# Six units' fronts of a graph layer's edge loop moved into the mixing stage

## The chip, the cores and the metric

One core of one Trainium2 chip runs the whole kernel in one launch. The metric is the device time of an execution in microseconds (us); the median over runs is compared. The kernel is written in Bass: each engine (TensorE, VectorE, ACT, GpSimd, and SyncE, which only issues transfers) has its own instruction list and runs it in order, and engines wait for each other on semaphores.

## What is computed

A graph layer in float32 on 3125 nodes with 256 channels and 50000 edges sorted by their destination: a message layer over the edges, an attention-like mixing, and a mixture of experts. What matters here:

```python
xn  = layernorm(x)
msg = silu(concat(xn[src], xn[dst], w) @ mW1 + mb1)        # edge loop, front
msg = layernorm(msg) * g + b                               # statistics: front; scaling: back
msg = silu(msg @ mW2 + mb2)                                # back
agg = segment_sum(msg, src, N)                             # back
y   = silu(concat(xn, agg) @ uW1 + ub1) @ uW2 + ub2        # hpre = xn @ uW1[:256] + ub1
mix = (q @ (k^T v)) / N @ Wout + bout                      # folded: mixed = xn @ mixG
x   = x + xn + y + mix                                     # then the experts
```

(The kernel's `near` side is the node whose block a tile of edges shares, `dst_table` holds the other side.)

## The kernel before, in words

Nodes are 25 blocks of 125. The product of `xn` with the near half of `mW1` stands in SBUF (`src_hi`, `src_lo`, high and low part), that with the far half in the DRAM table `dst_table`. The matrices of attention are folded into one 256x256 matrix `mixG`.

**Mixing stage** (TensorE L1004 to L1024). Blocks come in seven chunks `CH` of 4, 4, 4, 4, 4, 4 and 1 (numbered 0 to 6). For each block TensorE makes `mixed` = xn @ mixG (six matmuls, banks 0 and 1 in turn), and waits from block 2 on for VectorE's addition of the block two back (L1695, L1696); behind the blocks of a chunk it makes `hpre` (twelve matmuls, banks 2 to 5, two a chunk), which ACT copies out with a bias (L1327 to L1333). From chunk 2 on TensorE waits for the copy of the chunk two back. GpSimd meanwhile issues the twelve gathers of units 0 to 5 (L777 to L780), waits for the end of mixing, clears `agg` (L783, over `xnT_lo`, which mixing reads) and only then starts its part of the loop. SyncE writes `row_list` and `weight_rows` to DRAM (L597 to L601), waits for these (L602) and for `w2_lo` (L603), which VectorE writes after mixing (L1758, L1759), and then loads `near_rows` and the weight rows of `hotT`, five units at a time (L604 to L614). `near_rows` lies over `w2c`, from which `w2_hi` and `w2_lo` are made.

**Edge loop** (an `edge_step(n, k, ...)` on each engine, L1033, L1335, L1701 and `edge_pair` L767). 212 units of 2x128 edges. Step n does, in this order on each engine:

- TensorE: tr, the transposes of unit n-6; the second-layer products of n-7; the near products of unit n (four matmuls that pick rows of `src_hi` and `src_lo` by the one-hot `hotT`, L1069, bank 1 or 2); the sums of n-8.
- ACT: copy of the transposes (n-6), SiLU in place on `msg1` (n-1, L1346), scaling `msg1n` (n-5, L1353), SiLU of the second layer (n-7, L1360).
- VectorE: `hotT` of unit n+1 (L1708), shifts `nw_b` of a pair (n-4), the first addition into `agg` (n-9), `msg1T_lo` (n-6), the second addition (n-9), statistics of n-1 (L1743), the addition of the near products of unit n to the gathered far rows (L1748), the one-hot `hot` (n-7).
- GpSimd, for pairs m, m+1: waits for both units' statistics (`spread_ok`), an addition and a power (L748, L750), then the four gathers of units m+6 and m+7.

The first 20 units and the last are written out, between them runs a hardware loop of ten units a turn. Before the loop TensorE waits for `w2_lo`, for all 25 additions of mixing and for all hpre copies.

The front of a unit is its `hotT`, near products, addition, SiLU and statistics; none of them touches `agg`, `msg1n`, or banks 3 to 6 and 0 and 7, which the back half uses. Before, the front of units 0 to 5 ran alone, ahead of the first tr.

## Time and profile before

| what | value |
|---|---|
| three runs | 1538.51, 1540.53 (median), 1542.70 us |
| the profiled execution | 1532.65 us, its span 1530.9 us, mean granted clock of TensorE 0.918 |
| busy, share of the span | TensorE 85%, its weight loads 74%, VectorE 75%, ACT 59%, GpSimd 57% |
| chain that ended last | TensorE 51%, VectorE 15%, ACT 11%, "issue" 10%, unknown 7% |
| mixing stage | 370.5 to 413.7 us from the start |
| first near product, first transposes of the loop | 419.45 and 431.07 us |

PE is TensorE, PEld its weight loads, DVE VectorE, POOL GpSimd, SP SyncE. A row of the timeline gives start, duration, engine, line, operation, output<-inputs, shape and count, and in brackets how long the engine had been idle and what ended that. A releaser "remote" or "another core or an unknown queue" is none that the profile knows; "issue" is an engine that waited for nothing the profile shows. A clock of 1.00 is TensorE's upper level (2.4 GHz), 0.50 its lower one (1.2 GHz).

### The profile page before, as it was taken

The page shows a single profiled execution, that of the slowest core. Times are in us where ns is not written, and L with a number is a line of the kernel's source. Part 1 is how long each engine was busy: PE and PEld are TensorE (multiplying, and loading weights), DVE is VectorE, ACT ScalarE, POOL GpSimd, SP SyncE. Part 2 cuts the span into 40 slices and gives each one's busy share as a digit, 9 for nine tenths or more (in the row PEclk, how much of TensorE's full clock was granted, in tenths as well). Part 3 has the DMA queues.
Part 4 walks back from the last instruction along what each step waited for, and adds up shares of the span by engine and source line. Part 5 has one row for each costly group of instructions (what it writes and reads, how often), then busy time and mean ns, then how long its engine had stood idle before and what let it go on. Part 6 is the DMA issues. An engine that isn't in the chain of part 4 may idle for free.

```text
span 1530.9 us, 31977 instructions
## 1 busy us (share of the span) xinstructions
PE 1302.3 (85%) x8639; PEld 1135.4 (74%) x8640; DVE 1154.1 (75%) x2784; ACT 904.1 (59%) x1796; POOL 866.8 (57%) x960
## 2 busy tenths in 40 slices
PE   2576727998789999999999999999998956999991
PEld 1365626887678888888888888888886745888891
DVE  6975815884279989999999999999994678766662
ACT  1843603442257777777777777777774553666660
POOL 2287870002277777777777777777760012676761
PEclk7676967998879999999999999999999987999996
DMA  3911100001123333333333333333354143444447
GB/s 131 163 27 25 43 14 8 15 3 41 41 87 103 94 93 93 93 102 97 90 93 93 102 93 94 92 95 100 94 66 165 41 149 138 66 72 75 73 64 265
DMA packets 69786, 129.87 MB, mean 85 GB/s; under 512 B 22626, under 2 KB 43424, under 8 KB 69095
## 3 DMA queue, kind: packets, MB, share of 16 engines
q0 software_dynamic: 35408, 74.18, 20.5%
q1 hardware_dynamic: 33538, 51.70, 11.7%
q10 hardware_dynamic: 780, 3.24, 0.5%
q8 instruction: 31, 0.51, 0.1%
q14 instruction: 29, 0.24, 0.1%
HBM read 103.71 MB, written 25.22 MB: 84 GB/s over the span
## 4 chain that ended last, share of the span: by engine, by line
PE 51%; DVE 15%; ACT 11%; issue 10%; another core or an unknown queue 7%; DMA 3%; DVEq 1%; ACTq 1%; POOLq 0%; SPq 0%
PE ps L840 9%; ACT msg1n_t L1353 7%; PE ps L1079 5%; PE ps L1057 3%; PE ps L1052 3%; PE ps L1053 3%; PE ps L1069 3%; PE ps L1180 2%; DVE place_val_t L1591 2%; PE ps L1209 2%; PE ps L1211 2%; PE ps L1210 2%; PE ps L1181 2%; PE ps L1182 2%
## 5 line engine op out<-in xcount | busy, mean ns | idle before, releaser
L763 POOL DMA_INDIRECT msg_t<-dst_table,stage_idx x424 | 422.7, 997 | 121.1 <-issue 119.5
L1052 PE MATMUL ps<-w_hi_t,msg1T_hi_t 128*128 128x256 f32 x848 | 239.3, 304 | 0.0
L1353 ACT ACTIVATE msg1n_t<-msg_t,nw_b,nw_y 128x256 f32<-128x256 f32 x424 | 229.3, 591 | 0.0
L1079 PE MATMUL ps<-msg_t,hot_t 128*125 128x256 f32 x848 | 222.4, 384 | 2.0 <-issue 0.9
L1053 PE MATMUL ps<-w_lo_t,msg1T_hi_t 128*128 128x256 f32 x848 | 221.6, 283 | 0.0
L1360 ACT ACTIVATE msg_t<-ps 128x512 f32<-128x512 f32 x212 | 125.5, 592 | 124.0 <-remote 100.6
L1748 DVE TENSOR_TENSOR msg_t<-ps,msg_t 128x512 f32<-128x512 f32 x212 | 144.4, 681 | 63.3 <-remote 59.4
L1726 DVE TENSOR_TENSOR agg_t<-agg_t,ps 125x256 f32 x424 | 173.6, 409 | 6.8 <-PE ps L1079 3.4
L1057 PE MATMUL ps<-w_hi_t,msg1T_lo_t 128*128 128x256 f32 x848 | 171.0, 283 | 0.0
L1053 PEld LDWEIGHTS ps<-w_lo_t,msg1T_hi_t 128*128 128x128 f32 x848 | 163.1, 192 | 0.0
L1341 ACT ACTIVATE msg1T_hi_t<-ps 128x512 fp32r<-128x512 f32 x212 | 126.4, 596 | 60.4 <-PE ps L840 56.0
L1052 PEld LDWEIGHTS ps<-w_hi_t,msg1T_hi_t 128*128 128x128 f32 x848 | 161.9, 191 | 0.0
L1079 PEld LDWEIGHTS ps<-msg_t,hot_t 128*125 128x125 f32 x848 | 143.4, 187 | 21.0 <-issue 6.4
L840 PEld LDWEIGHTS ps<-ident,msg1n_t 128*128 128x128 f32 x848 | 97.4, 141 | 75.6 <-ACT msg1n_t L1353 52.4
L840 PE MATMUL ps<-ident,msg1n_t 128*128 128x128 f32 x848 | 134.6, 282 | 21.7 <-ACT msg1n_t L1353 19.1
L729 POOL DMA_INDIRECT sorted_edges<-sort_sb_t,chunk_to x112 | 128.0, 1143 | 37.3 <-issue 32.6
L1743 DVE BATCH_NORM_STATS2 est<-msg_t 128x6 f32<-128x512 f32 x212 | 147.5, 696 | 2.1 <-ACT msg_t L1346 2.1
L1735 DVE SCALAR_TENSOR_TENSOR msg1T_lo_t<-ps,msg1T_hi_t 128x512 fp32r<-128x512 f32 x212 | 144.4, 681 | 4.6 <-issue 2.4
L1346 ACT ACTIVATE msg_t<-msg_t 128x512 f32<-128x512 f32 x212 | 133.7, 631 | 12.4 <-DVE msg_t L1748 11.4
L1057 PEld LDWEIGHTS ps<-w_hi_t,msg1T_lo_t 128*128 128x128 f32 x848 | 132.1, 192 | 0.0
L1069 PE MATMUL ps<-src_hi_t,hotT_t 127*128 x424 | 114.3, 290 | 8.4 <-DVE hotT_t L1708 8.4
L831 POOL DMA_INDIRECT total<-slot_z,to_row x56 | 88.6, 1582 | 48.9 <-ACT slot_z L1433 44.3
(373 smaller groups left out, 3098.8 us busy)
## 6 DMA issues: line engine op xcount, KB each, us to landing
near_rows<-row_list SPq DMA_DIRECT2D x42, 320.0 KB
w_sb_t<-in_L_ffn_W_dram SPq DMA_DIRECT2D x16, 512.0 KB, 8.7
msg_t<-dst_table,stage_idx POOLq DMA_INDIRECT x424
res_t<-in_x_dram SPq DMA_DIRECT2D x1, 3125.0 KB
total<-zero_chunks_t SPq DMA_DIRECT2D x1, 3125.0 KB
dst_table<-dst_stage SPq DMA_DIRECT2D x25, 125.0 KB
xm_table<-xm_t POOLq DMA_DIRECT2D x5, 625.0 KB, 7.6
sum_a_t<-total SPq DMA_DIRECT2D x5, 625.0 KB, 10.7
```

The source lines that it names most:

```text
L763: pool.indirect_dma_start(out=msg1[:, k, j, :], out_offset=None, in_=dst_table, in_offset=bass.IndirectOffsetOnAxis(stage_idx[:, G * k + j ...
L840: return pe.transpose(out_, in_, ident[0:rows, 0:rows])
L1052: pe.matmul(o[j], part(msg1T_hi, j, c), w2_hi[:, c, :], start=(c == 0), stop=False)
L1053: pe.matmul(o[j], part(msg1T_hi, j, c), w2_lo[:, c, :], start=False, stop=False)
L1057: m = pe.matmul(o[j], part(msg1T_lo, j, c), w2_hi[:, c, :], start=False, stop=(c == KD - 1))
L1069: m = pe.matmul(bank(1 + k % 2, D, first=j * D), hotT[0:HR, k, j * 128:j * 128 + 128], table[0:HR, bass.ts(blk[k, j], 1), :].rearrange("p ...
L1079: m = pe.matmul(bank(7 * (kl % 2), D, rows=NP, first=j * D), hot[:, kl % 2, j, 0:NP], msg2[:, kl % 2, j, :], start=True, stop=True)
L1353: m = A(msg1n[:, (kl + 1) % 2, j, :], msg1[:, kk, j, :], ACT.Identity, bias=nw_b[:, kk, j:j + 1], scale=nw_y[:, kk, j:j + 1])
L1726: dve.tensor_tensor(a, a, bank(7 * ((k + 1) % 2), D, rows=NP, first=j * D), ALU.add).then_inc(sum_sb, 1)
L1735: dve.scalar_tensor_tensor(msg1T_lo[:, k % 2], bank(3 + k % 2), 1.0 / ROOT_D, msg1T_hi[:, k % 2].bitcast(F32), ALU.add, ALU.subtract).then ...
L1743: dve.bn_stats(est_pairs[:, kk, :], msg1[:, kk].rearrange("p j n -> p n j")).then_inc(spread_ok, 1)
L1748: dve.tensor_tensor(v, bank(1 + k % 2), v, ALU.add).then_inc(pre_sb, 1)
```

## The change

The fronts of units 0 to 5 are issued within mixing: unit 0 in chunk 2, units 1 and 2 in chunk 3, 3 and 4 in chunk 4, 5 in chunk 5 (`FRONT`), on TensorE between the chunk's mixed and hpre products, on VectorE behind the chunk's additions, on ACT ahead of the chunk's hpre copy, but for unit 5's step there (SiLU of unit 4, scaling of unit 0), which stays behind the last copy. Mixing takes banks 0 and 7, hpre 3 to 6, so that 1 and 2 are the near products' own. `w2_hi` and `w2_lo` are made ahead of mixing, and TensorE waits for them there. GpSimd does its first two pairs (units 0 to 3) before it waits for the end of mixing and clears `agg`. Only positions, waits and bank numbers change; every product, addition and transfer is the same.

```diff
--- before.py
+++ after.py
@@ -462,6 +462,8 @@
         N_DST = [(NB + 1) // 2, NB // 2]
         SMALL = 9
         CH = [list(range(t, min(t + 4, NB))) for t in range(0, NB, 4)]
+        EARLY = 6
+        FRONT = {c: {2: [0], 3: [1, 2], 4: [3, 4], 5: [5]}.get(c, []) for c in range(len(CH))}
         LAST = UNITS + 9 + LAG
         FROM = 2
         PEEL = (UNITS // TURN - 1) * TURN
@@ -778,11 +780,12 @@
                 stage(m, m, 0)
             for m in range(AHEAD_UNITS):
                 gather(m)
-            pool.wait_ge(hpre_ps, len(CH))
-            pool.wait_ge(mixed_ps, NB)
-            pool.memset(agg[:], 0.0).then_inc(fills, 1)
             pool.wait_ge(token_ok, 1)
             for m in range(0, FROM * TURN, 2):
+                if m == EARLY - 2:
+                    pool.wait_ge(hpre_ps, len(CH))
+                    pool.wait_ge(mixed_ps, NB)
+                    pool.memset(agg[:], 0.0).then_inc(fills, 1)
                 edge_pair(m, m % TURN, m // TURN)
             with pool.Fori(FROM, UNITS // TURN - 1) as i:
                 st.enter(i, FROM, len(PARTS) + TURN // 2)
@@ -1001,33 +1004,6 @@
                 m.then_inc(mixG_ps, 1)
 
 
-            pe.wait_ge(w_lo_ok, MIXG_LO)
-            for c, blocks in enumerate(CH):
-                t0, nb = blocks[0], len(blocks)
-                for t in blocks:
-                    if t >= 2:
-                        pe.wait_ge(mixed_ok, t - 1)
-                    o = bank(t % 2, D, rows=NP)
-                    for k in range(KD):
-                        pe.matmul(o, xnT_hi[:, t, k, 0:NP], mixG_hi[:, k, :], start=(k == 0), stop=False)
-                        pe.matmul(o, xnT_hi[:, t, k, 0:NP], mixG_lo[:, k, :], start=False, stop=False)
-                        m = pe.matmul(o, xnT_lo[:, t, k, 0:NP], mixG_hi[:, k, :], start=False, stop=(k == KD - 1))
-                    m.then_inc(mixed_ps, 1)
-                if c >= 2:
-                    pe.wait_ge(hpre_sb, c - 1)
-                for f in range(KD):
-                    o, F = bank(2 + 2 * (c % 2) + f, nb * 128), slice(f * 128, f * 128 + 128)
-                    for k in range(KD):
-                        pe.matmul(o, uw1x_hi[:, k, F], xnT_hi[:, t0:t0 + nb, k, :], start=(k == 0), stop=False)
-                        pe.matmul(o, uw1x_lo[:, k, F], xnT_hi[:, t0:t0 + nb, k, :], start=False, stop=False)
-                        m = pe.matmul(o, uw1x_hi[:, k, F], xnT_lo[:, t0:t0 + nb, k, :], start=False, stop=(k == KD - 1))
-                m.then_inc(hpre_ps, 1)
-
-
-            pe.wait_ge(w_lo_ok, W2_LO)
-            pe.wait_ge(bw_in, 128)
-            pe.wait_ge(mixed_ok, NB)
-            pe.wait_ge(hpre_sb, len(CH))
             blk = {}
 
             def edge_step(n, k, turn_weights):
@@ -1080,7 +1056,35 @@
                                       start=True, stop=True)
                     m.then_inc(sum_ps, 1)
 
-            for n in range(FROM * TURN):
+            pe.wait_ge(w_lo_ok, W2_LO)
+            pe.wait_ge(bw_in, 128)
+            for c, blocks in enumerate(CH):
+                t0, nb = blocks[0], len(blocks)
+                for t in blocks:
+                    if t >= 2:
+                        pe.wait_ge(mixed_ok, t - 1)
+                    o = bank(7 * (t % 2), D, rows=NP)
+                    for k in range(KD):
+                        pe.matmul(o, xnT_hi[:, t, k, 0:NP], mixG_hi[:, k, :], start=(k == 0), stop=False)
+                        pe.matmul(o, xnT_hi[:, t, k, 0:NP], mixG_lo[:, k, :], start=False, stop=False)
+                        m = pe.matmul(o, xnT_lo[:, t, k, 0:NP], mixG_hi[:, k, :], start=False, stop=(k == KD - 1))
+                    m.then_inc(mixed_ps, 1)
+                if c >= 2:
+                    pe.wait_ge(hpre_sb, c - 1)
+                for n in FRONT[c]:
+                    edge_step(n, n % TURN, 16)
+                for f in range(KD):
+                    o, F = bank(3 + 2 * (c % 2) + f, nb * 128), slice(f * 128, f * 128 + 128)
+                    for k in range(KD):
+                        pe.matmul(o, uw1x_hi[:, k, F], xnT_hi[:, t0:t0 + nb, k, :], start=(k == 0), stop=False)
+                        pe.matmul(o, uw1x_lo[:, k, F], xnT_hi[:, t0:t0 + nb, k, :], start=False, stop=False)
+                        m = pe.matmul(o, uw1x_hi[:, k, F], xnT_lo[:, t0:t0 + nb, k, :], start=False, stop=(k == KD - 1))
+                m.then_inc(hpre_ps, 1)
+
+
+            pe.wait_ge(mixed_ok, NB)
+            pe.wait_ge(hpre_sb, len(CH))
+            for n in range(EARLY, FROM * TURN):
                 edge_step(n, n % TURN, 16 * (n // TURN) + 16)
             with pe.Fori(FROM, UNITS // TURN - 1) as i:
                 for k in range(TURN):
@@ -1323,15 +1327,6 @@
             for c in range(KD):
                 act.wait_ge(mixG_ps, c + 1)
                 A(mixG_hi[:, c, :], bank(2 + c, D), ACT.Copy, scale=1.0 / N).then_inc(mixG_sb, 1)
-            act.wait_ge(small_in, 16 * SMALL)
-            for c, blocks in enumerate(CH):
-                act.wait_ge(hpre_ps, c + 1)
-                for f in range(KD):
-                    m = A(hpre[:, blocks[0]:blocks[0] + len(blocks), f, 0:NP],
-                          bank(2 + 2 * (c % 2) + f, len(blocks) * 128).rearrange("p (i n) -> p i n", n=128)[:, :, 0:NP],
-                          ACT.Identity, bias=ub1_col[:, f:f + 1])
-                m.then_inc(hpre_sb, 1)
-
             def edge_step(n, k, turn_rows):
                 late, kl = n - LAG, (k - LAG) % TURN
                 m_ = late - 6
@@ -1360,8 +1355,20 @@
                     A(msg2[:, (kl + 1) % 2].rearrange("p j n -> p (j n)"), bank(5 + (kl + 1) % 2), ACT.Silu)\
                         .then_inc(msg2_sb, 1)
 
+            act.wait_ge(small_in, 16 * SMALL)
+            for c, blocks in enumerate(CH):
+                for n in FRONT[c]:
+                    if n < EARLY - 1:
+                        edge_step(n, n % TURN, 32)
+                act.wait_ge(hpre_ps, c + 1)
+                for f in range(KD):
+                    m = A(hpre[:, blocks[0]:blocks[0] + len(blocks), f, 0:NP],
+                          bank(3 + 2 * (c % 2) + f, len(blocks) * 128).rearrange("p (i n) -> p i n", n=128)[:, :, 0:NP],
+                          ACT.Identity, bias=ub1_col[:, f:f + 1])
+                m.then_inc(hpre_sb, 1)
+
             pairs = 0
-            for n in range(FROM * TURN):
+            for n in range(EARLY - 1, FROM * TURN):
                 edge_step(n, n % TURN, 32 * ((n - LAG) // TURN) + 32)
             with act.Fori(FROM, UNITS // TURN - 1) as i:
                 pairs = TURN // 2 * i
@@ -1691,10 +1698,9 @@
                 dve.wait_ge(mixG_sb, c + 1)
                 dve.scalar_tensor_tensor(mixG_lo[:, c, :], bank(2 + c, D), 1.0 / N, mixG_hi[:, c, :].bitcast(F32),
                                          ALU.mult, ALU.subtract).then_inc(w_lo_ok, 1)
-            for t in range(NB):
-                dve.wait_ge(mixed_ps, t + 1)
-                dve.tensor_tensor(res[R, t, :], res[R, t, :], bank(t % 2, D, rows=NP), ALU.add).then_inc(mixed_ok, 1)
-
+            step(dve.tensor_scalar(w2_hi[:], w2c[:], ROOT_D, None, ALU.mult))
+            dve.scalar_tensor_tensor(w2_lo[:], w2c[:], ROOT_D, w2_hi[:].bitcast(F32), ALU.mult, ALU.subtract).then_inc(w_lo_ok, 1)
+            dve.wait_ge(table_sb, LOADS)
 
             blk = {}
 
@@ -1753,14 +1759,17 @@
                     dve.tensor_tensor(hot[:, (k + 1) % 2, :, 0:NP], iota[:, 1:NP + 1].unsqueeze(1).broadcast_to([128, G, NP]),
                                       rows.broadcast_to([128, G, NP]), ALU.is_equal).then_inc(hot_ready, 1)
 
-            dve.wait_ge(mixG_sb, KD)
-
-            step(dve.tensor_scalar(w2_hi[:], w2c[:], ROOT_D, None, ALU.mult))
-            dve.scalar_tensor_tensor(w2_lo[:], w2c[:], ROOT_D, w2_hi[:].bitcast(F32), ALU.mult, ALU.subtract).then_inc(w_lo_ok, 1)
-            dve.wait_ge(table_sb, LOADS)
             near_of = lambda n: 16 * ((n + 1) // TURN) + 16
             pairs = 0
-            for n in range(-1, FROM * TURN):
+            for c, blocks in enumerate(CH):
+                for t in blocks:
+                    dve.wait_ge(mixed_ps, t + 1)
+                    dve.tensor_tensor(res[R, t, :], res[R, t, :], bank(7 * (t % 2), D, rows=NP), ALU.add).then_inc(mixed_ok, 1)
+                for n in FRONT[c]:
+                    if n == 0:
+                        edge_step(-1, TURN - 1, -1, near_of(-1), 0)
+                    edge_step(n, n % TURN, n // TURN, near_of(n), 32)
+            for n in range(EARLY, FROM * TURN):
                 edge_step(n, n % TURN, n // TURN, near_of(n), 32 * (n // TURN) + 32)
             with dve.Fori(FROM, UNITS // TURN - 1) as i:
                 pairs = TURN // 2 * i
```

## Rows read from the trace of the kernel before

**Rows 1.** Busy time by stage: us; PE, PEld, DVE, ACT, POOL; PEclk; DMA

```profile
500.00:534.00 34.00, 33.06 (x234) 29.33 (x233) 31.70 (x75) 25.55 (x51) 25.72 (x31) 1.00 0.32 95
```

**Rows 2.** Timeline of TensorE between mixing and the loop

```profile
413.39 0.27 PE L1023 MATMUL ps<-xnT_lo_t,uw1x_hi_t 128*128 128x128 f32 x1
419.45 0.58 PE L1069 MATMUL ps<-src_hi_t,hotT_t 127*128 x1 [5.78 <-DVE hotT_t L1708]
431.07 1.12 PE L840 MATMUL ps<-ident,msg1n_t 128*128 128x128 f32 x4 [2.08 <-ACT msg1n_t L1353]
```

**Rows 3.** The same timeline, the other engines

```profile
413.21 0.69 DVE L1759 SCALAR_TENSOR_TENSOR w_lo_t<-w2c,w_hi_t 128x512 fp32r<-128x512 f32 x1
413.70 0.62 ACT L1330 ACTIVATE hpre_t<-ps,ub_col 128x125 f32<-128x125 f32 x2 [0.74 <-PE ps L1023]
413.73 5.43 POOL L783 MEMSET agg_t<- 128x6400 f32 x1 [26.14 <-PE ps L1023]
413.98 0.35 SPq L608 DMA_DIRECT2D near_rows<-row_list  x1
421.43 0.63 ACT L1346 ACTIVATE msg_t<-msg_t 128x512 f32<-128x512 f32 x1 [5.80 <-DVE msg_t L1748]
422.09 0.71 DVE L1743 BATCH_NORM_STATS2 est<-msg_t 128x6 f32<-128x512 f32 x1 [0.44 <-ACT msg_t L1346]
422.71 0.67 DVE L1748 TENSOR_TENSOR msg_t<-ps,msg_t 128x512 f32<-128x512 f32 x1
```

**Rows 4.** The line of hotT (L1708) in 413 to 420: duration ns min/median/max

```profile
L1708 DVE TENSOR_SCALAR hotT_t<-near_rows,row_col x2: 334/804/1274, 418.0 to 419.2; 125x256 fp32r<-125x256 f16 x2
```

**Rows 5.** Timeline of the mixing stage

```profile
370.41 7.27 SPq L600 DMA_DIRECT2D weight_rows<-side_w_t  x2
388.32 0.42 DVE L1696 TENSOR_TENSOR res_t<-res_t,ps 125x256 f32<-125x256 f32 x1 [8.13 <-remote]
388.80 0.57 PE L1012 MATMUL ps<-mixG_hi,xnT_hi_t 128*125 128x256 f32 x1 [5.31 <-DVE res_t L1696]
394.79 1.25 ACT L1330 ACTIVATE hpre_t<-ps,ub_col 128x500 f32<-128x500 f32 x2 [9.48 <-PE ps L1023]
408.76 0.39 PE L1021 MATMUL ps<-xnT_hi_t,uw1x_hi_t 128*128 128x512 f32 x1
408.96 0.42 DVE L1696 TENSOR_TENSOR res_t<-res_t,ps 125x256 f32<-125x256 f32 x1 [0.29 <-PE ps L1014]
411.51 0.28 PE L1012 MATMUL ps<-mixG_hi,xnT_hi_t 128*125 128x256 f32 x1
```

**Rows 6.** DMA queues (packets, MB, share) in 387:388, then in 388:392

```profile
q1 hardware_dynamic: 53, 0.03, 8.7%
...
q0 software_dynamic: 58, 0.16, 11.6%
```

**Rows 7.** Busy time by stage again, PEclk third from the end

```profile
391.00:392.00 1.00, 1.00 (x6) 1.00 (x5) 0.07 (x1) 0.00 (x0) 0.00 (x0) 0.50 0.00 0
392.00:393.00 1.00, 1.00 (x6) 0.78 (x6) 0.36 (x1) 0.00 (x0) 0.00 (x0) 1.00 0.00 0
...
414.00:419.00 5.00, 0.00 (x0) 0.00 (x0) 0.97 (x1) 1.61 (x3) 5.00 (x1) 0.69 0.42 135
```

**Rows 8.** Chain of waits: four near products at the lower and upper clock

```profile
438.04 0.85 PE ps L1069 x4
...
455.95 0.48 PE ps L1069 x4
```

**Rows 9.** TensorE's sequencer, loads of block numbers (L491), duration ns

```profile
L491 PEldq TENSOR_LOAD <-tile_blk x106: 328/332/527, 414.5 to 1141.3; - x106
```

**Rows 10.** The page's group of gathers: busy, mean ns, idle before

```profile
L763 POOL DMA_INDIRECT msg_t<-dst_table,stage_idx x424 | 422.7, 997 | 121.1 <-issue 119.5
```

**Rows 11.** Timeline in the loop: GpSimd's power and an addition beside it

```profile
693.65 1.04 POOL L750 TENSOR_TENSOR nw_y<-nw_v,minus_half 128x4 f32<-128x4 f32 x1
693.94 0.69 DVE L1748 TENSOR_TENSOR msg_t<-ps,msg_t 128x512 f32<-128x512 f32 x1 [0.71 <-remote]
```

## The prediction

> **What bounds the kernel now.** In what follows near(u), silu(u) and add(u) are unit u's near products, its SiLU and the addition of the near products to the gathered rows, and tr(u) the transposes that open its back half. I read the stage table first: in the settled loop TensorE is busy 33.06 of 34 us at full clock [rows 1]. What reaches the loop later by x makes the program x longer, and what the change does to the loop's own pace is nothing, since no instruction of the loop body changes. So only the joint between the mixing stage and the loop is open. There the last hpre product ends at 413.39+0.27 = 413.66, near(0) starts at 419.45, tr(0) at 431.07 [rows 2]: 17.41 us between the end of mixing and tr(0), in which TensorE does six sets of near products and otherwise waits. The other engines' rows say for what [rows 3]: w2_lo ends, SyncE issues near_rows at 413.98, VectorE can write hotT(0) at 418.0 [rows 4]. Then each unit goes round add 0.67, SiLU 0.63, statistics 0.71, add, since the statistics stand ahead of the next addition in VectorE's order, about 2 us a unit. Then GpSimd's power and ACT's scaling follow.
>
> The mixing stage itself is TensorE's, but for one stall: VectorE stood idle for 8.13 us ahead of its ninth addition, and TensorE stood 5.31 us for it [rows 5].
>
> **Start of mixing.** The two w2c operations (the longer takes 0.69 [rows 3]) and their wait go ahead of mixing, which begins later by at most 2x0.69 = 1.4 us. Cover: the 5.31 us for which TensorE stood before block 10 [rows 5]. If that stall is gone too, near(0) still waits for something later than the end of that stall's chunk (next part). So 0; without both covers 1.4.
>
> **near(0), the term that I had to choose most in.** near_rows used to be held back by w2_lo. Now SyncE's wait ahead of it, for the weight_rows writes (issued from 370.41 on [rows 5]), counts. Their queue q1 still moved 53 packets in 387 to 388, and in 388 to 392 only the gathers' q0 moved [rows 6]. So near_rows is issued at about 388.1. From issue to hotT it took 418.0-413.98 = 4.05 us [rows 3, 4]; hotT 0.34, hand-over 0.15: near(0) at 392.65. TensorE has chunk 2's mixed products done at about 391.8 (the chunk's end, 394.6 below, less 2.75 for its hpre products) whatever the W2 move does, and waits. The clock is at 0.50 there and was back at 1.00 at 392 only after TensorE had run without a break since 388.80 [rows 5, 7]. The new 1 us hole comes into that stretch, so I take near(0) at the low level, 0.85 instead of 0.48 [rows 8], and a quarter of the twelve hpre products too. Those take 411.51-408.76 = 2.75 us at full clock [rows 5], 2.75x0.85/0.48 = 4.87 at the low one, so 0.75x2.75+0.25x4.87 = 3.28. Chunk 2 ends at 392.65+0.85+3.28 = 396.8, where it ended at 394.79-0.2 = 394.6 (its ACT copy [rows 5]): **+2.2 us**. Ends: +1.3 (all at full clock) and +5.8 (completion of the writes seen 2 us late, all twelve slow).
>
> **near(1) to near(5)**: 5x0.48 [rows 8] = **+2.4 us**; nothing else can hide them, TensorE is the busy one in these chunks. In chunks 3 and 4 the second unit's hotT is written only after the chunk's last addition: 0.29+0.42 for that [rows 5], 0.34 and 0.15, less 0.48 for the unit ahead: 0.72 twice, **+1.45 us**. TensorE's sequencer loads block numbers at even units, 0.33 us each [rows 9]; that of unit 0 hides in the wait, two count, **+0.66**. VectorE's words load at unit 0 is hidden by chunk 2's hpre products.
>
> VectorE's moved work, two units a chunk, is 2x(0.34+0.71+0.67), with a SiLU of 0.63 between, some 4.1 us [rows 3, 4]; it stands beside 2x0.48+2.75 = 3.7 us of near and hpre products and the next chunk's first two mixed products, for TensorE's wait is for the addition two blocks back. So 0; without those two blocks 0.4 a chunk. ACT's moved SiLUs stand ahead of the hpre copies; these have a whole chunk until their bank is used again. GpSimd's first two pairs move in: each four gathers of 0.997+0.29 [rows 10] and 1.04 for the power [rows 11], about 6.5 us with the small ones. They fall into chunks 4 and 5, end about 2 us before mixing does, and memset starts as before. The third SyncE load waits for hotT(5) and comes early. Cost of these 0.
>
> **After mixing.** The SiLU of unit 4 stays behind the last hpre copy in ACT's order, VectorE's statistics(4) wait for it, and behind these stand add(5) and block 24's addition, for which TensorE waits with nothing else it may do: 0.62+0.63+0.71+0.67+0.42 [rows 3, 5] and 0.1 of hand-overs = 3.15 us. msg1n(0) is scaled meanwhile. So tr(0) comes 3.15 us after the end of mixing, not 17.41: **-14.26 us**.
>
> **memset beside VectorE.** Its 5.43 us [rows 3] now stand beside these operations. In the trace hotT(0) began at 418.0 under the memset and took 1.27 instead of 0.34, till just behind the memset's end [rows 3, 4], while an addition under GpSimd's power took its 0.69 [rows 11]. So I let only hotT(7) wait, some 2 us; it stands behind block 24's addition, and add(6), whose SiLU is wanted a step later, gets under 1 us later. Cost 0, ends 0 and 1. The Trainium skill, SBUF — State Buffer, section "SBUF: two separate sides", makes this sharper: the port pair of VectorE and GpSimd is an exclusive lock, taken by VectorE for two-port forms (or two SBUF inputs against a GpSimd operation that reads SBUF), and the loser waits for the whole instruction. By that rule the hotT row is explained, and statistics(4) and both additions would run free; the sum stays. Only the rival below, where everything is held, would contradict it.
>
> Sum: -14.26+2.2+2.4+1.45+0.66 = **-7.5 us**. The profiled execution took 1532.65, so 1525.1 on its scale; the runs' median is 1540.53, 7.9 above it, and as the comparison will be of such medians, I take 1540.53-7.5 = **1533.0**. The loop's ramp behind tr(0) is left as it was. 0.3% (4.6 us) is about what can be told from no change.
>
> **Rivals.**
> A, *everything VectorE does is held by the memset*. Then statistics(4) starts at 5.5 us behind the end of mixing and tr(0) at 5.5+0.71+0.67+0.42+0.1 = 7.4: 4.25 lost, 1537.3. For: nothing of VectorE ran under this memset but hotT, which was held. Against: [rows 11]. Chance 0.09.
>
> B, *near(0) late and slow*: the upper end above, +5.8 instead of +2.2, gives 1536.6. For: the writes' last packets are not their completion; and twelve products are done at the low clock if it is slow to rise. Against: VectorE's stall ended at 388.32, as if the traffic had ended. Chance 0.15.
>
> C, **slower**, *VectorE is starved while GpSimd issues gathers*. The 8.13 us stall has no releaser in the profile, only gathers and weight_rows ran, and it ended when they did. Place: the two new bursts of four gathers, in chunks 4 and 5, where VectorE now has much more to do and TensorE waits for its hotT. Twice 8.1 gives 16.2-7.5 = 8.7 slower, 1549.2; it decides from 12.1 us of such stalls on. Against: one stall in twelve gathers, its cause may be weight_rows alone, and the same bursts stood beside the ramp before without one. The Trainium skill, Runtime: NRT & Kernel Launch, section "Instruction fetch mechanics", says that engines load code in blocks of 256 instructions by DMA, mostly hidden; no row shows whether that made this stall. Chance 0.08.
>
> D, *more than forecast*: the clock stays up across the 3.15 us hole and in chunk 2 (in 414 to 419, a hole of 5.8 us, it fell to 0.50 in time to give a mean of 0.69 [rows 7]). Three steps of the ramp save 0.37 each on near products, chunk 2 its 0.9: -9.5, 1531.0. Chance 0.13.
>
> That the change has no effect because GpSimd becomes the bound I leave out: its third pair starts behind the memset, 5.5 us after mixing, and what it gives is wanted two units behind tr(0), which is later.
>
> **How the numbers follow.** The forecast has 0.55, spread 2 us about 1533. A to D have 0.45. Faster by over 0.3%: forecast but for its edge (0.51) and D, 0.64. Within: A, B, the edge, 0.28. Slower: C, 0.08. Range: from D less the 2 us by which the runs differ, 1528.5, up through A and B with as much on top, 1540.5; C and little else is left out.
>
> **What would show it.** Right: near_rows issued at 388, near(0) at 392.7, mixing ends at about 420.4, tr(0) 3 us later at 423.5, spacing behind it as before. The TensorE hole behind mixing 3 us against 5.8, and the silu, statistics and additions of units 0 to 4 inside 393 to 415. Wrong: near(0) behind 394 (B), statistics(4) not straight behind its SiLU (A), an additions row with several us of idle time and no releaser in chunks 3 to 5 (C), a loop of another length between tr(0) and the last sum, for which I have no mechanism.

## The result, and the profile after

The changed kernel took **1532.72 us** (median of 18 runs, 1523.7 to 1540.13) against 1541.1 us for the kernel before in the same comparison (18 runs, 1536.01 to 1553.66): ratio **0.9929, 95% interval 0.991 to 0.9948**, faster by less than 1%. Two further comparisons gave 0.9923 (0.99 to 0.9946) and 0.9934 (0.9909 to 0.996). The forecast was 1533.0 us, a ratio of 1533.0/1540.53 = 0.9951, just above that interval. Ratios and intervals here are estimates from all runs of both kernels, and differ by up to 0.002 from the quotient of the two medians, which is 0.9946 here.

The two first profiles can't be subtracted end to end. That of before took 1532.65 us, less than any of its 18 timed runs; that of after took 1540.13, as much as the slowest. Before any instruction that the change touches, the second was already 375.36-369.61 = 5.75 us late (second copy of mixG). So all that follows is counted from that copy, or by stretches.

Page of the changed kernel, its head and the groups that answer to [rows 10]:

```profile
span 1538.4 us, 31979 instructions
...
PE 1301.8 (85%) x8639; PEld 1132.1 (74%) x8640; DVE 1156.0 (75%) x2784; ACT 902.4 (59%) x1796; POOL 865.7 (56%) x960
...
L765 POOL DMA_INDIRECT msg_t<-dst_table,stage_idx x424 | 422.3, 996 | 120.5 <-issue 119.8
```

Timeline of its mixing stage, chunk 2 (answers to [rows 5] and [rows 3]):

```profile
375.36 0.39 ACT L1329 ACTIVATE mixG_hi<-ps 128x256 fp32r<-128x256 f32 x1 [1.34 <-PE ps L1002]
376.15 7.21 SPq L602 DMA_DIRECT2D weight_rows<-side_w_t  x2
377.31 0.38 PE L1068 MATMUL ps<-mixG_hi,xnT_hi_t 128*125 128x256 f32 x1 [1.99 <-DVE w_lo_t L1702]
390.70 0.42 DVE L1767 TENSOR_TENSOR res_t<-res_t,ps 125x256 f32<-125x256 f32 x1 [3.13 <-remote]
392.40 0.94 POOL L765 DMA_INDIRECT msg_t<-dst_table,stage_idx  x1 [0.30 <-issue]
393.96 0.35 SPq L610 DMA_DIRECT2D near_rows<-row_list  x1
394.94 0.42 DVE L1767 TENSOR_TENSOR res_t<-res_t,ps 125x256 f32<-125x256 f32 x1 [3.82 <-issue]
395.41 0.58 PE L1068 MATMUL ps<-mixG_hi,xnT_hi_t 128*125 128x256 f32 x1 [3.27 <-issue]
395.76 1.25 ACT L1365 ACTIVATE hpre_t<-ps,ub_col 128x500 f32<-128x500 f32 x2 [9.75 <-remote]
400.48 0.58 PE L1045 MATMUL ps<-src_hi_t,hotT_t 127*128 x1 [0.86 <-DVE hotT_t L1714]
```

and behind mixing:

```profile
428.73 5.43 POOL L788 MEMSET agg_t<- 128x6400 f32 x1 [2.78 <-PE ps L1081]
429.22 0.63 ACT L1341 ACTIVATE msg_t<-msg_t 128x512 f32<-128x512 f32 x1
429.88 0.70 DVE L1749 BATCH_NORM_STATS2 est<-msg_t 128x6 f32<-128x512 f32 x1 [5.68 <-ACT msg_t L1341]
430.50 0.67 DVE L1754 TENSOR_TENSOR msg_t<-ps,msg_t 128x512 f32<-128x512 f32 x1
431.09 0.41 DVE L1767 TENSOR_TENSOR res_t<-res_t,ps 125x256 f32<-125x256 f32 x1
431.42 2.89 DVE L1714 TENSOR_SCALAR hotT_t<-near_rows,row_col 125x256 fp32r<-125x256 f16 x1
431.55 0.66 PE L843 MATMUL ps<-ident,msg1n_t 128*128 128x128 f32 x4 [2.88 <-DVE res_t L1767]
```

How long an engine was held has to be read against its input. The idle time ahead of an addition also holds VectorE's ordinary wait for the product, 3.0 us behind the twelve hpre products. So "held" means below only that part of the idle time in which the product was ready (start of the addition, less the end of the last of its six products). In the kernel before, the product of block 8 was ready at 382.50+0.28 = 382.78,

```profile
382.50 0.28 PE L1014 MATMUL ps<-mixG_hi,xnT_lo_t 128*125 128x256 f32 x1
```

and its addition began at 388.32: of the 8.13 us of idle time 5.54 are a hold. Summed over the additions of chunks 1 and 2 VectorE was held for 7.0, 6.9 and 7.8 us in the three profiles of the kernel before, and for 8.8, 8.2 and 8.8 in the three of the changed kernel, in the first two of these in several pieces of up to 4 us. The idle times alone (8.1 and 3.8 us in the first two profiles) look as if the change had halved it.

The fence behind mixing is the chain of the forecast, row for row: silu(4), statistics(4), add(5), block 24's addition, tr(0), 2.88 us after TensorE's last product. hotT(7) alone is held, until the memset ends at 434.16.

The stretches of three profiles of each kernel (first one, then the repeats in the experiments; us between rows of the timelines; unit n is the transposes' copy of that unit on ScalarE):

| stretch | before | changed |
|---|---|---|
| mixG copy to end of mixing | 44.06, 43.98, 44.23 | 53.31, 50.71, 52.77 |
| end of mixing to tr(0) | 17.40, 17.38, 17.39 | 2.88, 2.89, 2.89 |
| tr(0) to unit 20 | 72.1, 71.7, 72.2 | 69.9, 70.5, 69.7 |
| unit 20 to unit 211 | 658.8, 662.5, 663.1 | 666.9, 666.2, 668.4 |
| unit 211 to the end | 368.9, 368.4, 368.0 | 370.0, 369.0, 367.8 |

Means: mixing +8.2, behind it -14.5, first steps of the loop -2.0, loop +5.7, rest +0.5.

### The profile page after: what moved, and what is told of

Read it like the earlier page. It is cut to its first block, busy times and chain, and to the rows that moved or that the text cites. A ratio compares the mean times of both kernels' runs of the same rounds, so it can differ in the third digit from the quotient of the medians.

```text
span 1538.4 us, 31979 instructions
## 1 busy us (share of the span) xinstructions
PE 1301.8 (85%) x8639; PEld 1132.1 (74%) x8640; DVE 1156.0 (75%) x2784; ACT 902.4 (59%) x1796; POOL 865.7 (56%) x960
## 4 chain that ended last, share of the span: by engine, by line
PE 50%; DVE 14%; ACT 12%; another core or an unknown queue 10%; issue 9%; DMA 3%; ACTq 1%; DVEq 1%; POOLq 0%
PE ps L843 8%; ACT msg1n_t L1348 8%; PE ps L1055 6%; PE ps L1033 3%; PE ps L1028 3%; PE ps L1045 3%; PE ps L1029 3%; DVE place_val_t L1598 2%; PE ps L1184 2%; PE ps L1213 2%; PE ps L1215 2%; PE ps L1214 2%; PE ps L1185 2%; PE ps L1186 2%
## 5 line engine op out<-in xcount | busy, mean ns | idle before, releaser
L1336 ACT ACTIVATE msg1T_hi_t<-ps 128x512 fp32r<-128x512 f32 x212 | 126.4, 596 | 58.1 <-PE ps L843 52.4
L752 POOL TENSOR_TENSOR nw_y<-nw_v,minus_half 128x4 f32<-128x4 f32 x106 | 111.0, 1047 | 8.6
```

## The experiments

Three jobs of four kernels, each job on one chip with its own runs of the kernel before (medians 1543.21, 1533.04 and 1543.4 us). Ratios are to these, with 95% intervals. They are compared within a job; the changed kernel itself did not run in the second job.

### Repeating the changed kernel

> The changed kernel once more, unchanged, for a second profile. In the first one the stretch from the transposes' copy of unit 20 to that of unit 211 took 666.9 us, against 658.8 us before the change, although no instruction of the loop differs. Theory (the loop's pace wanders from one execution to the next, by some us): the second profile gives another length, 655 to 668, with no relation to the change, while mixing (second mixG copy to last hpre product) stays at 53 us and tr(0) stays 2.9 us behind its end. Rival (the change shifts GpSimd's or the loads' phase against the loop and makes it longer): again 665 to 669, and the ratio to the kernel before comes out at 0.993 only because the stages ahead of the change are quicker. Ratio by both 0.991 to 0.996.

Measured 1530.17 us, ratio 0.9923 (0.99 to 0.9946). Loop 666.2 us, mixing 50.7, tr(0) 2.89 behind it. So the loop's length came out as the rival said, and mixing 2.6 us shorter than in the first profile, where TensorE's wait in the stall was 2.71 instead of 3.27 us and TensorE was back at the upper clock by 390. The stall comes back (its last piece is shown), VectorE and ScalarE being released together:

```profile
382.60 0.94 POOL L765 DMA_INDIRECT msg_t<-dst_table,stage_idx  x1 [0.30 <-issue]
384.07 0.35 SPq L610 DMA_DIRECT2D near_rows<-row_list  x1
385.82 1.25 ACT L1365 ACTIVATE hpre_t<-ps,ub_col 128x500 f32<-128x500 f32 x2 [9.48 <-remote]
385.89 0.75 DVE L1767 TENSOR_TENSOR res_t<-res_t,ps 125x256 f32<-125x256 f32 x2 [3.27 <-remote]
386.37 0.58 PE L1068 MATMUL ps<-mixG_hi,xnT_hi_t 128*125 128x256 f32 x1 [2.71 <-DVE res_t L1767]
```

### The SiLU of unit 4 earlier

```diff
                 for n in FRONT[c]:
                     if n < EARLY - 1:
                         edge_step(n, n % TURN, 32)
+                    else:
+                        silu(n, n % TURN)
                 act.wait_ge(hpre_ps, c + 1)
```

> One part alone added: ScalarE issues the SiLU of unit 4 ahead of the hpre copies of chunk 5 instead of behind the last ones. Theory (the hole behind mixing is the chain last hpre copy, silu(4), statistics(4), add(5), addition of block 24): silu, statistics and add(5) then lie in chunks 5 and 6, what is left of 2.9 us is the last hpre copy or the addition of block 24, some 0.8 to 1.0 us, and tr(0) comes 2.0 us earlier against the end of mixing; the program is 1 to 2 us faster than the changed kernel, ratio to the kernel before about 0.992. Rival (tr(0) early is no use, since add(6), silu(6) and the roots of pair 4 behind the memset set the pace of the first steps): hole shorter by 2 us, but unit 10 at the same time as in the changed kernel, ratio as for it.

Measured 1530.01 us, ratio 0.9927 (0.9897 to 0.9957), no different from the changed kernel. tr(0) came 1.78 us behind mixing, so only 1.1 us of the 2.0 were had: the next thing in the way is msg1n(0), which lies where uw1x_hi lay and so can't be scaled before the last hpre product; behind the last hpre copy, it takes another 1.08 us. From mixing's end unit 10 came 37.57 us later, against 37.94 in the repeat of the changed kernel, so only 0.4 of the 1.1 us were left by then.

```profile
421.79 0.62 ACT L1371 ACTIVATE hpre_t<-ps,ub_col 128x125 f32<-128x125 f32 x2 [0.74 <-PE ps L1081]
422.30 1.08 ACT L1352 ACTIVATE msg1n_t<-msg_t,nw_b,nw_y 128x256 f32<-128x256 f32 x2
423.53 0.63 PE L843 MATMUL ps<-ident,msg1n_t 128*128 128x128 f32 x4 [1.78 <-ACT msg1n_t L1352]
```

### near_rows issued before the writes are complete

```diff
-            sp.wait_ge(side_out, 48)
             sp.wait_ge(w_lo_ok, W2_LO)
+            sp.wait_ge(rows_out, 16)
+            for h in range(2):
+                load_near(h, h * NEAR, NEAR)
+            sp.wait_ge(side_out, 32)
```

(row_list's write has a semaphore of its own, rows_out; load_near is the near_rows load of the loop.)

> near_rows is issued straight behind the weight_rows writes, waiting only for the write of row_list; the load of the weights still waits for all writes. Theory (near(0) was held by the completion of the weight_rows writes, by way of near_rows, hotT): the load of near_rows no longer waits 17.8 us for them; it is done by the time they are, hotT(0) is written in chunk 2 without waiting, and near(0) waits for the weights' load alone, some 2 us behind the writes instead of 6; chunk 2 ends 2 to 4 us earlier, mixing takes 49 to 51 us instead of 53.3, ratio to the kernel before 0.990 to 0.991. Rival (the two 320 KB loads queue behind the writes and the gathers and delay them): writes complete later by as much as the loads take, near(0) no earlier, mixing 53 us, ratio as for the changed kernel.

Measured 1532.96 us, ratio 0.9945 (0.9915 to 0.9976). near_rows was issued at 376.08 instead of some 386, the weights' load at 386.58, and near(0) still began at 392.60, 24.6 us behind the mixG copy (25.1, 24.6 and 24.7 in the changed kernel); mixing took 52.75 us. Neither theory: the writes were not delayed (17.74 us from issue to completion), near(0) simply no longer depended on them. What it waits for is in its row:

```profile
388.34 0.75 DVE L1774 TENSOR_TENSOR res_t<-res_t,ps 125x256 f32<-125x256 f32 x2 [4.67 <-remote]
392.60 0.57 PE L1052 MATMUL ps<-src_hi_t,hotT_t 127*128 x1 [0.86 <-DVE hotT_t L1721]
```

The four additions of chunk 2 stand ahead of hotT(0) on VectorE, and they come late by the stall.

### The front one chunk later

```diff
-        FRONT = {c: {2: [0], 3: [1, 2], 4: [3, 4], 5: [5]}.get(c, []) for c in range(len(CH))}
+        FRONT = {c: {3: [0, 1], 4: [2, 3], 5: [4, 5]}.get(c, []) for c in range(len(CH))}
```

> The six units moved one chunk later: units 0 and 1 in chunk 3, 2 and 3 in chunk 4, 4 and 5 in chunk 5, none in chunk 2. Theory (near(0) in chunk 2 costs its wait and twelve products at the low clock, 4 us or so): chunk 2 has no wait for hotT, mixing takes 49 to 50.5 us instead of 53.3, chunk 5 gets 1.2 us longer by its second unit, and behind mixing the hole stays below 4 us; ratio to the kernel before 0.990 to 0.992. Rival (the stall of VectorE and TensorE ahead of block 10 would cost these us anyway, and TensorE only waits elsewhere): mixing 52 to 53 us, ratio as for the changed kernel.

Measured 1531.59 us, ratio 0.9938 (0.9915 to 0.9961), mixing 52.2 us: the rival. Moving near(0) out of the stall's chunk saves nothing in all: TensorE waits for the stall anyway (5.50 us ahead of block 10 here), and chunks 3 and 5, with a second unit each, took 0.5 and 1.9 us longer.

### The kernel before, again

> The kernel before once more, unchanged, for a second profile. All five profiles of changed kernels have 666 to 667 us from the transposes' copy of unit 20 to that of unit 211, the one of the kernel before 658.8. Theory (that one profile is a quick one, as its time of 1532.65 against a median of 1541 says, and the change leaves the loop's pace alone): this profile shows 664 to 668 us. Rival (the change costs the loop 8 us, and gains these elsewhere): 657 to 661 us. Ratio 1.000 within 0.003.

Measured 1534.35 us against 1533.04 (ratio 1.0008, 0.9991 to 1.0026). Loop 662.5 us: midway between the two ranges, so it decides nothing. The stall is the same as in the first profile: VectorE 8.10 us, TensorE 5.26.

### Gathers held back

```diff
             for m in range(AHEAD_UNITS):
+                if m == 1:
+                    pool.wait_ge(mixed_ps, 12)
                 gather(m)
```

> The changed kernel with GpSimd's gathers of units 1 to 5 held back until mixed product 12 is done, so that they are not in flight beside the weight_rows writes. Theory (the stall of VectorE and ScalarE without a releaser ends one to two microseconds behind the weight_rows writes in every profile; the writes are slow because the gathers share the DMA engines): the writes complete well before 17.8 us after their issue, say 8 to 14, the stall ahead of block 8's addition is gone or under 1 us and TensorE doesn't stand for it (2.7 to 5.6 us so far); near(0) comes 3 us or more earlier. Against it the gathered rows of units 1 to 5 come up to 15 us late for their additions, so the whole is no faster, ratio 0.992 to 0.998. Rival (the writes alone take that time and cause the stall): completion at 17 to 18 us again, stall unchanged.

Measured 1524.19 us, ratio 0.9946 (0.9933 to 0.9958). In its timeline chunks 1 and 2 go through without a hold, each addition beginning 0.04 us behind its product; the hold is now in chunk 3, under the last of the ten gathers (384.11 to 395.34):

```profile
380.97 1.25 ACT L1367 ACTIVATE hpre_t<-ps,ub_col 128x500 f32<-128x500 f32 x2 [4.34 <-PE ps L1083]
381.67 0.42 DVE L1769 TENSOR_TENSOR res_t<-res_t,ps 125x256 f32<-125x256 f32 x1 [3.03 <-PE ps L1072]
383.57 0.35 SPq L610 DMA_DIRECT2D near_rows<-row_list  x1
387.81 0.57 PE L1047 MATMUL ps<-src_hi_t,hotT_t 127*128 x1 [3.97 <-DVE hotT_t L1716]
394.42 0.42 DVE L1769 TENSOR_TENSOR res_t<-res_t,ps 125x256 f32<-125x256 f32 x1 [4.66 <-issue]
397.44 0.42 DVE L1769 TENSOR_TENSOR res_t<-res_t,ps 125x256 f32<-125x256 f32 x1 [2.60 <-remote]
```

The 4.66 us of idle time in the fifth row are no hold: that product ended at 394.38, late since TensorE had waited for near(0). The last row is one. The product of block 13 was ready at 395.10, and its addition began at 397.44, 2.10 us behind the last gather's issue; VectorE was held for 2.7 us in all, and TensorE stood 2.04 us ahead of block 15 for it. So the stall goes where the gathers go. Why ten of them held VectorE for 2.7 us here, and twelve for 7 to 10 us earlier in the stage, is not shown.

The writes took 15.4 us from issue to completion in place of 17.8, not 8 to 14. With the stall gone from chunk 2, near(0) did wait for near_rows: the mechanism of the prediction, with 3.97 us where it had about 1. near(0) came 20.5 us behind the mixG copy, 4 us earlier, but mixing took 52.9 us all the same, by this wait and by the hold in chunk 3.

### The writes first

```diff
             load_table()
-            sp.wait_ge(mixG_ps, KD)
-            sp.dma_start(uw1_sb[:], uW1[D:2 * D, :].rearrange("(k p) n -> p k n", p=128)).then_inc(uw1_in, 16)
             sp.wait_ge(w_hi_ok, ROWS_HI)
...
+            sp.wait_ge(mixG_ps, KD)
+            sp.dma_start(uw1_sb[:], uW1[D:2 * D, :].rearrange("(k p) n -> p k n", p=128)).then_inc(uw1_in, 16)
             sp.wait_ge(side_out, 48)
```

> The changed kernel with SyncE's order altered: row_list and weight_rows are written as soon as their data are there (359.3 in the second profile), ahead of SyncE's wait for the mixG products that held them until 366. Theory (the completion of these writes pins near(0), and the stall of VectorE and ScalarE is bound to the same traffic): the writes are complete at about 375 to 378, near_rows is loaded before chunk 2, the stall before block 8's or 9's addition shrinks from 3 to 6 us to under 1, near(0) doesn't wait; mixing takes 46 to 48 us instead of 50.7 to 53.3, and the program is 3 to 6 us faster than the changed kernel: ratio to the kernel before 0.988 to 0.990. Rival (code loading or something else holds VectorE at that place whatever the writes do): near(0) earlier, but the stall remains with its 3 to 6 us, mixing 50 us or more, ratio 0.991 to 0.993.

Measured 1524.61 us, ratio 0.9942 (0.9927 to 0.9957). near_rows was issued at 371.24, long before chunk 2, and the stall did not change (VectorE held for 8.3 us in all). The rival was right that these writes have no part in it:

```profile
371.24 0.35 SPq L610 DMA_DIRECT2D near_rows<-row_list  x1
385.93 0.95 POOL L765 DMA_INDIRECT msg_t<-dst_table,stage_idx  x1 [0.30 <-issue]
389.06 0.75 DVE L1767 TENSOR_TENSOR res_t<-res_t,ps 125x256 f32<-125x256 f32 x2 [6.69 <-remote]
389.53 0.58 PE L1068 MATMUL ps<-mixG_hi,xnT_hi_t 128*125 128x256 f32 x1 [5.61 <-DVE res_t L1767]
393.32 0.58 PE L1045 MATMUL ps<-src_hi_t,hotT_t 127*128 x1 [0.86 <-DVE hotT_t L1714]
```

Mixing took 52.4 us, and near(0) came 24.4 us behind the mixG copy, hardly earlier than in the changed kernel. With no gather beside them before 370.42 the writes were complete within 12.0 us of their issue (359.27 to 371.24), so two thirds of the 17.8 us are their own. Between 361 and 369, where they run alone, their queue keeps the 16 DMA engines 14% busy, as much as two of them at full load.

### W2, banks and the early load without the front

EARLY = 0 and an empty FRONT in the changed kernel; all twelve first units run behind mixing.

> The change without its front: the six units' first halves run behind mixing as before, but W2's split, the early near_rows load and the new banks stay. Theory (the front inside mixing is what pays, the early load alone gives its 4 us and hotT(0)): mixing takes 45 to 47 us (44.1 before, plus the W2 wait), tr(0) comes 12.0 to 13.5 us behind its end instead of 17.4, the ratio is 0.996 to 0.998. Rival (nearly all comes from the early load, the front only moves work of TensorE about): tr(0) at most 10 us behind the end of mixing, ratio 0.993 to 0.994 as for the whole change.

Measured 1530.96 us, ratio 0.9996 (0.9983 to 1.001): no gain, less than either theory gave. Mixing took 46.06 us and tr(0) came 14.57 behind it, 60.6 us behind the mixG copy against 61.5 before. near(0) did come early, 1.60 us behind the last product instead of 5.78, but the memset, which used to run while near_rows was loaded, now lies over the first two units:

```profile
413.20 5.43 POOL L788 MEMSET agg_t<- 128x6400 f32 x1 [28.19 <-PE ps L1081]
415.47 0.69 DVE L1754 TENSOR_TENSOR msg_t<-ps,msg_t 128x512 f32<-128x512 f32 x1 [2.68 <-PE ps L1045]
416.07 2.71 DVE L1714 TENSOR_SCALAR hotT_t<-near_rows,row_col 125x256 fp32r<-125x256 f16 x1
418.70 0.68 DVE L1749 BATCH_NORM_STATS2 est<-msg_t 128x6 f32<-128x512 f32 x1
```

TensorE waited 3.02 us for the hotT in the third row. In the same job two kernels with the front gave 0.9946 and 0.9942 (the two experiments above), so the change's gain is the front's.

### Before and after on one chip

> The kernel before once more, in the same job as the changed one, to settle the length of the loop (unit 20 to unit 211). Profiles so far: 658.8, 662.5 and 659.3 us for the kernels without a front in mixing, 666 to 667 for those with one in the first two jobs, but 661.1 for one with a front in the third job, whose kernels before were 10 us quicker. Theory (the loop's length goes with the job, not with the change): this profile and that of the changed kernel in this job lie within 3 us of each other. Rival (the front in mixing makes the loop longer): 5 to 8 us apart.

Measured 1545.4 us (ratio 1.0, 0.9968 to 1.0032), loop 663.1 us.

> The changed kernel in the same job. Loop from unit 20 to unit 211 within 3 us of the kernel before in this job (theory) or 5 to 8 us longer (rival). Mixing 50.5 to 53.5 us with a stall of VectorE of 3 to 6 us that ends 1.5 to 3.5 us behind the issue of the twelfth gather; tr(0) 2.9 us behind mixing; ratio 0.992 to 0.995.

Measured 1532.47 us, ratio 0.9934 (0.9909 to 0.996); mixing 52.8, tr(0) 2.89 behind it, VectorE's idle time in the stall 6.78 us. Loop 668.4 us, 5.3 longer than before on the same chip, which is the rival's figure.

### Writes first and gathers spaced out

```diff
             for m in range(AHEAD_UNITS):
+                if m:
+                    pool.wait_ge(mixed_ps, 3 * m)
                 gather(m)
```

together with the SyncE order of "The writes first".

> The changed kernel with both: the weight_rows writes first (near(0) then waits for nothing), and the gathers of unit m held until mixed product 3m is done, so that they go out two at a time and not twelve in a row. Theory (VectorE and ScalarE are held until the burst of gathers is through; it takes the burst, two or four at a time do nothing of the kind in the edge loop): no idle time without a releaser above 1.5 us on VectorE in mixing, TensorE never waits 2 us or more, mixing takes 43.8 to 46.5 us instead of 50.7 to 53.3, the program is 5 to 8 us faster than the changed kernel, ratio to the kernel before 0.987 to 0.990. Rival (the stall is tied to that place of VectorE's program and came out smaller with late gathers by chance): 3 us or more of it remain ahead of block 8 or 9, mixing above 48 us, ratio 0.991 to 0.994.

Measured 1525.4 us, ratio **0.987** (0.9828 to 0.9912). The twelve gathers went out in groups of four, two, four and two, from 376.63 to 399.68, not strictly in pairs. Mixing took 43.5 us, front and all, as short as before the change, which had no front but 7 us of stall; VectorE waits for products only, every addition up to block 23 beginning 0.04 us behind its product (0.11 for the first):

```profile
389.45 0.42 DVE L1769 TENSOR_TENSOR res_t<-res_t,ps 125x256 f32<-125x256 f32 x1 [3.01 <-PE ps L1072]
392.48 0.38 PE L1047 MATMUL ps<-src_hi_t,hotT_t 127*128 x1 [0.86 <-issue]
```

The ratio is at the lower end of what the theory gave, the stall is gone as it said. Against the changed kernel in this job the median is 7.1 us lower, with six runs only and intervals that just touch. Spaced gathers without the writes first, and spaced gathers in the kernel before, were not run; the stall costs the kernel before 7 us as well (chunk 2 took 12.7 us there, the chunks behind it 5.6), so this gain is not one of the front.

### And the early SiLU

> The same with the SiLU of unit 4 issued ahead of chunk 5's hpre copies. Theory: mixing as in the run before, tr(0) 1.8 us behind its end instead of 2.9 (the last hpre copy 0.62 and the scaling of unit 0, 1.08, which may not begin before the hpre products are done), the program up to 1.1 us faster, which the timing can hardly tell; ratio 0.986 to 0.990. Rival (the first steps absorb it): unit 10 at the same distance from the end of mixing as without it.

Measured 1520.61 us, ratio **0.9848** (0.9812 to 0.9883), tr(0) 1.78 us behind a mixing of 43.5 us. From mixing's end unit 10 came 36.82 us later here and 37.84 in the run before, so the 1.1 us are kept to unit 10. That the median is 4.8 us lower than without this edit is more than the edit can explain, and the ratio lies below the expected 0.986 to 0.990; the intervals overlap. This is the best version: on its chip 1520.6 us, against 1532.5 for the changed kernel and 1543.4 for the one before.

## Why the prediction was right, and where not

The direction came out, and so did the size of the first comparison: predicted -7.5 us, and its medians differ by 8.4 (10.9 by the ratio), those of the two repeats by 13.0 and 10.9. That the total lies so close is in part luck. The chain behind mixing was right by itself, but the profiles' stretches add up to -2.1 us, since mixing grew by 8.2 us in place of 6.7 and the loop's +5.7 was no term of the sum at all; what the timings show beyond that has no explanation in the profiles. The steps:

- **After mixing, -14.26**: measured 17.39 to 2.89, -14.5. Right in every row.
- **memset, cost 0**: hotT(7) was held for 2.89 us, statistics(4) and add(5) took their 0.70 and 0.67 under the memset, rival A is out. By the Trainium skill's page SBUF — State Buffer, section "SBUF: two separate sides" (an exclusive lock, the loser waiting for the whole instruction), the trace agrees here, and again in the kernel without the front, hotT 2.71 us. That kernel shows what the cost is where hotT stands ahead of work that is wanted: statistics(0) waited behind it. So the cost of 0 in the changed kernel goes by the position of hotT(7), behind everything that tr(0) needs.
- **Start of mixing, cost 0**: W2's wait put mixing 1.05 us later behind the mixG copy (0.90 to 1.95). It has no cover: the stall doesn't end at a fixed time, as I had it, but 1.6 to 1.7 us behind the last gather's issue in the kernel before and 2.5 to 3.4 in the changed one. In the two changed profiles where chunk 0 was partly at the lower clock, another 1.4 went there: from the first product to the chunk's copies 7.45 and 7.57 us, where the third and all of before have 6.0 to 6.1.
- **near(0), +2.2**: the *reason* failed. near_rows was issued 18.6 us behind the mixG copy (18.5 forecast), but near(0) came 25.1, 24.6 and 24.7 behind it and not 23.0, since hotT(0) stands behind chunk 2's four additions, and these behind the stall. The sum over chunks 1 and 2 was 21.34, 18.60 and 22.15 us against 18.27, 18.17 and 18.46: +3.1, +0.4 and +3.7. Their mean of 2.4 is nearly the forecast's size, by another way, which is luck. Without the stall, in the kernel with spaced gathers, chunk 2 took 7.25 us in place of an undisturbed chunk's 5.63, so near(0) by itself costs 1.6 (0.86 of it the wait for hotT(0)). The rest is the stall's: against chunks 1 and 2 without one it cost 7.0 to 7.3 us before, and 8.5, 5.8 and 9.3 in the changed kernel. TensorE's twelve hpre products were at the lower clock where the stall was long:

```profile
392.00:400.00 8.00, 4.34 (x20) 3.90 (x18) 2.03 (x6) 1.25 (x2) 1.04 (x2) 0.67 0.47 131
400.00:408.00 8.00, 7.52 (x34) 6.57 (x34) 2.13 (x6) 1.88 (x3) 0.00 (x0) 0.69 0.00 0
```

(busy time by stage of the changed kernel, columns as in [rows 7]). The wait for near_rows is real only once the stall is gone: 3.97 us with late gathers.
- **near(1) to near(5) and their waits, 2.4+1.45+0.66 = 4.5**: in the kernel with spaced gathers chunks 3 and 4 take 7.27 us each in place of 5.63, chunk 5 6.13 in place of 5.65, together 3.8; in the three profiles of the changed kernel it is 3.7 to 3.8. The wait for the second hotT was 0.39 us, not 0.72. The block-number loads cost nothing: that of unit 2 ran from 408.60 to 408.95 beside products that show no gap.
- **"The loop's ramp is left as it was"**: tr(0) to unit 20 got 2.0 us shorter.
- **"A loop of another length, for which I have no mechanism"**: this is open. The unit 20 to 211 stretch was 658.8, 662.5, 663.1 and 659.3 us in the four profiles without a front; 666.2 to 668.4 in all seven with a front and twelve gathers in a row; 661.1, 664.6 and 664.2 in the three with a front and late or spaced gathers. My theory of chips fell with the pair of the third job. Busy time by stage over that stretch, the kernel before in that job:

```profile
510.00:1173.00 663.00, 643.27 (x4566) 575.23 (x4564) 599.49 (x1419) 494.23 (x951) 488.17 (x591) 1.00 0.35 99
```

and the changed kernel in the same job:

```profile
493.00:1162.00 669.00, 643.64 (x4572) 575.36 (x4571) 600.74 (x1421) 494.76 (x953) 490.12 (x592) 1.00 0.35 98
```

The work and the clock are the same, TensorE stands idle 25.4 us instead of 19.7, in small holes. One reading is that the front leaves GpSimd's gathers and roots in another phase to the other engines; nothing here shows it. One profile a kernel, and single stretches of ten units that vary by a microsecond or two, don't settle it.
- Also open, the total: by the means of the table, with the stretch from the key loop's end to the mixG copy (which no edit touches, 13.4 against 11.5), the profiles give the change 4 us, the timings 8 to 13. The rest is in execution-to-execution variation ahead of it (that loop ended between 354.6 and 355.7 us in eleven profiles and between 362.8 and 364.2 in three, of both kinds) or in what single profiles don't sample.

Rival B's number (1536.6) was not met, though its mechanism of a late near(0) was partly true. Rival C's stall of VectorE under gathers exists, but the bursts of four in chunks 4 and 5 did nothing; its price of 8.1 us was the whole idle time, of which 5.54 were a hold. The Trainium skill, Runtime: NRT & Kernel Launch, section "Instruction fetch mechanics", says that an engine's code is loaded by DMA in blocks of 256 instructions, at a cost that is mostly hidden. Code packets are in the trace: in the repeat of before one is in the queues in 372 to 376,

```profile
q8 instruction: 1, 0.02, 1.9%
```

a second one (q14) in 377 to 378, and none between 378 and 400, while the idle time of 8.10 us runs from 379.2 to 387.3. The same two are there in the two kernels with spaced gathers, where nothing was held (383 to 385 and 376 to 377). So no row ties the stall to code loading; whether an engine got its code late all the same can't be seen. That the gathers cause the stall is shown, how they do it is open. Rival D (clock stays up behind mixing) held only for the hole: 1.00 in 424 to 432, but 0.57 in 432 to 440, where the first steps of the loop are.

## What to carry over

An idle row without a releaser belongs to something: move each suspect by itself and see which one takes the stall along. And count as stalled only the time in which the input was ready. Here twelve gathers in a row held VectorE for 7 to 10 us, ScalarE as well, and issuing them in groups of two to four, tied to the progress of the stage they run beside, shortened that stage by 9 us and the program by 7, as much as the whole change was to give. When a step is moved into another stage, look at what stands ahead of it in its engine's order there, and not only at the transfer that it used to wait for.

## What the runs showed that was not expected

- Twelve gathers issued back to back (1.25 us apart) left VectorE idle beside a ready product for 6.9 to 9.7 us in all, the last hold ending 1.6 to 3.4 us behind the last gather's issue, in all eleven profiles that had them. ScalarE's copies came 2.0 to 2.7 us late in the kernel before and 4.4 to 6.8 in the changed one, there released within 1 us of VectorE. With the same gathers in groups of two to four there was nothing of the kind in two profiles of two.
- The two weight_rows writes (212 KB each) take 17.7 to 17.9 us from issue to completion beside the gathers, 15.4 beside two of them, and 11.9 to 12.0 in the three kernels that issue them ahead of the gathers.
- Clearing 128x6400 words on GpSimd (5.43 us) holds VectorE's comparison (hotT, 0.34 us alone) to the end of the clearing, 2.71 and 2.89 us, and neither its statistics nor its additions from PSUM.
